# Attention and feed-forward block on one core: turning the row maxima on VectorE, splitting q and k on GpSimd, and products that nobody reads

## The reference

```
h = layernorm(x) * (1 + ca) + sa
q, k, v = h @ w_qkv.T            16 heads of width 8
a = q @ k.T / sqrt(8)            512 x 512 for each head
z = a - max(a over keys)
s = 1 + z(1 + z/2 (1 + z/3))             where z >= 0
s = 1 / (1 - z(1 - z/2 (1 - z/3)))       elsewhere (z <= 0 here)
x = x + ga * ((s / sum(s)) @ v @ w_out.T + b_out)
h = layernorm(x) * (1 + cb) + sb
x = x + gb * ffn(h)              128 -> 512 -> 512 -> 128, relu, weights +1 or -1
```

## Time and profile before

| | |
|---|---|
| median of 3 runs | 790.41 us (789.8 to 790.81) |
| the profiled execution | 786.48 us |
| its span, first to last instruction | 784.6 us |
| busy share of the span | PE 83%, PEld 31%, DVE 84%, ACT 75%, POOL 75% |
| granted TensorE clock, mean | 0.915 |

### The profile page before, as it was taken

One profiled execution on the slowest core, in us unless ns is written; L12 is line 12 of the kernel. 1 busy time (PEld: TensorE's weight loads), 2 busy tenths in 40 slices (PEclk: granted clock), 3 DMA queues, 4 the chain that ended last, 5 costly groups with the idle time before them and its releaser, 6 DMA issues.

```text
span 784.6 us, 9551 instructions
## 1 busy us (share of the span) xinstructions
PE 654.2 (83%) x2897; PEld 242.1 (31%) x2897; DVE 660.6 (84%) x806; ACT 590.3 (75%) x539; POOL 584.9 (75%) x348
## 2 busy tenths in 40 slices
PE   4377777877889998899989898899879999997877
PEld 2132222222222343223322342234322342242244
DVE  6779999798989999999989998999989999985020
ACT  2036688686897889888888889888888889899411
POOL 6227697588976999589968997789967987889310
PEclk9555669677999999999999999999999999999989
DMA  4523112410233113411331123411341120001000
GB/s 147 169 77 126 42 49 81 151 50 12 64 90 129 46 49 98 155 48 50 98 117 47 48 61 83 151 48 49 85 155 48 48 78 16 8 9 45 13 18 13
DMA packets 41110, 56.35 MB, mean 72 GB/s; under 512 B 7852, under 2 KB 24516, under 8 KB 41060
## 3 DMA queue, kind: packets, MB, share of 16 engines
q1 hardware_dynamic: 40388, 54.44, 23.2%
q10 hardware_dynamic: 672, 1.31, 0.5%
HBM read 32.06 MB, written 18.89 MB: 65 GB/s over the span
## 4 chain that ended last, share of the span: by engine, by line
PE 44%; DVE 24%; issue 15%; ACT 14%; DMA 1%; ACTq 0%; DVEq 0%; POOL 0%; POOLq 0%
DVE mx L712 12%; PE MB L417 10%; DVE cub L701 9%; PE OP L499 8%; PE SA L478 8%; PE Z L458 7%; ACT prob L552 5%; ACT sq L541 5%; PE MB L426 3%; PE SA L417 2%; PE MB L391 2%; ACT hid L582 2%; PE SA L426 1%; PE MB L394 1%; PE MB L410 1%
## 5 line engine op out<-in xcount | busy, mean ns | idle before, releaser
L844 POOL TENSOR_TENSOR cub<-cub 128x2048 f32<-128x2048 f32 x128 | 460.3, 3604 | 111.4 <-DVE cub L701 111.4
L541 ACT ACTIVATE sq<-Z,shift 128x1024 f32<-128x1024 f32 x256 | 282.9, 1117 | 110.9 <-PE Z L458 108.8
L712 DVE TENSOR_REDUCE mx<-SA 128x2 f32<-128x1024 f32 (+1 forms) x278 | 307.0, 1105 | 35.9 <-PE SA L478 34.6
L701 DVE SCALAR_TENSOR_TENSOR cub<-sq,Z 128x1024 f32<-128x1024 f32 x256 | 309.5, 1210 | 12.1 <-ACT sq L541 10.8
L552 ACT ACTIVATE prob<-cub 128x2048 f32<-128x2048 f32 x128 | 244.2, 1910 | 0.0
L478 PE MATMUL SA<-KH,QL 64*128 64x512 f32 x496 | 145.7, 523 | 62.3 <-DVE mx L712 51.4
L458 PE MATMUL Z<-QH,KH 64*128 64x512 f32 x512 | 139.8, 536 | 28.9 <-DVE cub L701 28.0
L499 PE MATMUL OP<-prob,Vq 128*16 128x512 f32 x1024 | 145.1, 641 | 1.4 <-ACT OT L590 1.4
L458 PEld LDWEIGHTS Z<-QH,KH 64*128 64x128 f32 x512 | 52.5, 199 | 222.3 <-DVE cub L701 145.7
L417 PE MATMUL MB<-hid,W 128*128 128x512 f32 x216 | 119.3, 640 | 0.0
L478 PEld LDWEIGHTS SA<-KH,QL 64*128 64x128 f32 x496 | 56.6, 200 | 162.0 <-DVE mx L712 132.1
(11 more groups left out here) (113 smaller groups left out, 396.4 us busy)
## 6 DMA issues: line engine op xcount, KB each, us to landing
parts_q<-SQ SPq DMA_DIRECT2D x32, 256.0 KB, 2.6
QL<-parts_q SPq DMA_DIRECT2D x64, 128.0 KB, 2.7
QH<-parts_q SPq DMA_DIRECT2D x64, 128.0 KB, 2.8
KH<-parts_k SPq DMA_DIRECT2D x62, 128.0 KB, 2.7
parts_k<-SK SPq DMA_DIRECT2D x28, 256.0 KB, 2.6
nd<-OT SPq DMA_DIRECT2D x128, 32.0 KB
xa<-L_attn_x SPq DMA_DIRECT2D x8, 256.0 KB, 4.2
QH<-mp SPq DMA_DIRECT2D x128, 4.0 KB
```

The costliest lines, as they stand in the source:

```text
L541: nc.scalar.activation(sq[:, h, :], Z[:, h, :], ACT.Square, bias=shift[:, 0:1]).then_inc(s_sq, 1)
L701: nc.vector.scalar_tensor_tensor(cub[:, m % RING, h, :], sq[:, h, :], CUB_ADD, Z[:, h, :], ALU.add, ALU.mult).then_inc(s_cv, 1)
L712: nc.vector.tensor_reduce(to, unit_bank(m, u)[:, heads[0]:heads[-1] + 1, :], AX_X, ALU.max)\
L844: nc.gpsimd.tensor_tensor(ff, ff, ff, ALU.mult).then_inc(s_fp, 1)
```

## The change

- **Maxima.** PE's transposing product and `alone` are gone. In steps 1, 5, 9 and 13 DVE makes the coarse and the fine part from `mx` in SBUF into a new tensor `ms` ([128 x 16] each; the first behind the first cubic, the second behind the first reduction) and turns them over with its own transpose of 32 x 32 blocks behind the second cubic ([128 x 32] into `mp`). SP writes the rows with eight DMAs of 2 KB, each of 16 runs of 128 bytes, in place of four of 4 KB.
- **q and k.** From batch 1 on ACT copies q (and k) whole into the second slot of `SQ` (`SK`), and POOL makes both parts from it in steps 1 and 2: a multiply-add copy and a subtraction, [128 x 512] each. k's product moves from place "d" to place "c" of step 1, and POOL's copy of v for the third quad from step 1 to 3.
- **Normalising on POOL.** Mean times root is made first and its sign turned (two [128 x 4] operations more), and the [128 x 128] operations become multiply, then add.
- **Last batch.** x1, y, h2T, l0 and l1_0 of `MISC[7]` and the second roots (`rs2`) move up by up to one step; in the tail l1_1 is spread over steps 0 and 1 and l1_2 goes to step 4.
- **Products that nobody reads** (`fill`): up to two a step of [128 x 128] by [128 x 512], into `MB`, in steps 10 to 15 ahead of batch 0, in 13 steps of batch 0 and 10 of batch 1. v of batch 0 moves from step 13 to 2.

```
+MISC[FIRST] = [("hT", 1, [(0, "c", 4)]), ("q", 1, [(0, "d", 4)]), ("k", 1, [(1, "d", 4)]), ("v", 1, [(2, "c", 4)])]
+FILL = {(FIRST, n): ("v", 1) for n in range(10, H)}
+FILL |= {(0, n): ("k", 2) for n in range(2, 13)} | {(0, n): ("v", 2) for n in (14, 15)}
+FILL |= {(1, n): ("k", 3) for n in range(2, 8)} | {(1, n): ("x1", 1) for n in range(9, 13)}
-    ("x1", -1, [(8, "c", 4)]),
-    ("y", -2, [(9, "c", 1), (9, "d", 1), (10, "c", 1), (10, "d", 1)]),
-    ("h2T", -1, [(11, "d", 4)]),
+    ("x1", -1, [(8, "a", 4)]),
+    ("y", -2, [(9, "a", 1), (9, "c", 1), (9, "d", 1), (10, "a", 1)]),
+    ("h2T", -1, [(10, "d", 4)]),
-AT[B - 1] = MAIN_AT | {"w2g": 4, "mv2": 9, "rs2": 10, "x1n": 10}
+AT[B - 1] = MAIN_AT | {"w2g": 4, "st2": 8, "mv2": 8, "rs2": 9, "x1n": 9}
...
+            def fill():
+                if (b, n) in FILL:
+                    name, count = FILL[b, n]
+                    pe.wait_ge(s_taken[name], count)
+                    pe.wait_ge(s_wts, 1)
+                    nc.tensor.matmul(MB[:, :], ident[:, :], W1[:, n % KC, :], start=True, stop=True)
...
             m = s + AHEAD
             scores(s + 1, 0)
-            if alone(m):
-                logits(m, 0, (1,))
             misc("a")
-            logits(m, 1, (0, 1))
+            logits(m, 1)
             with_v(s)
             scores(s + 1, 1)
             misc("c")
-            maxima_across(m)
-            logits(m + 1, 0, (0,) if alone(m + 1) else (0, 1))
+            fill()
+            logits(m + 1, 0)
             misc("d")
+            fill()
...
+            def of_maxima(m, stage):
+                raw = mx[:, i, :].rearrange("p (e c) -> p e c", e=2)
+                if stage == 0:
+                    nc.vector.tensor_scalar(ms[:, i, :, 0, :], raw, -1.0, None, ALU.mult).then_inc(s_mh, 1)
+                elif stage == 1:
+                    nc.vector.scalar_tensor_tensor(ms[:, i, :, 1, :], raw, -1.0, ms[:, i, :, 0, :].bitcast(F32),
+                                                   ALU.mult, ALU.subtract).then_inc(s_ml, 1)
+                else:
+                    nc.vector.transpose(mp[:, i, :], ms[:, i].rearrange("p e a c -> p (e a c)").bitcast(F32))\
+                        .then_inc(s_mp, 1)
...
+                nc.gpsimd.tensor_tensor(nm[:, :], mv[:, :, 0], rs[:, :], ALU.mult).then_inc(s_nm, 1)
+                nc.gpsimd.tensor_scalar(nm[:, :], nm[:, :], -1.0, 0.0, ALU.mult, ALU.add).then_inc(s_nm, 1)
-                    last = nc.gpsimd.tensor_scalar(dst[:, t, :], src[:, t, :], mv[:, t, 0:1], rs[:, t:t + 1],
-                                                   ALU.subtract, ALU.mult)
+                    last = nc.gpsimd.tensor_scalar(dst[:, t, :], src[:, t, :], rs[:, t:t + 1], nm[:, t:t + 1],
+                                                   ALU.mult, ALU.add)
+            def parts_of(beta, name):
+                pool.wait_ge(s_taken[name], beta + 1)
+                nc.gpsimd.tensor_scalar(src[:, 0, :], src[:, 1, :].bitcast(F32), 1.0, 0.0, ALU.mult, ALU.add)\
+                    .then_inc(s_hi, 1)
+                nc.gpsimd.tensor_tensor(src[:, 1, :], src[:, 1, :].bitcast(F32), src[:, 0, :].bitcast(F32), ALU.subtract)\
+                    .then_inc(s_lo, 1)
...
-                    for a in range(PARTS):
-                        r = ROWS * e + R_MAX + a
-                        sp.dma_start(QH[r:r + 1, 2 * g:2 * g + 2, :].bitcast(F32), mp[2 * TB * e:2 * TB * (e + 1), quad % 2, a, :].bitcast(F32))\
+                    for k in range(P // 32):
+                        of = 32 * k + QUAD * TB * e
+                        sp.dma_start(rows_g[r:r + PARTS, :, :, k, :].bitcast(F32), mp[of:of + QUAD * TB, quad % 2, :])\
                             .then_inc(s_mrow[g], 16)
```

More of the change, by code:

```diff
@@ L55 @@
 LOADS = 4
+M_DMAS = 8
 FIRST = -1
@@ L74 @@
 ]
-MISC = {b: MAIN for b in range(FIRST, B - 1)}
+MISC = {b: MAIN for b in range(B - 1)}
+MISC[FIRST] = [("hT", 1, [(0, "c", 4)]), ("q", 1, [(0, "d", 4)]), ("k", 1, [(1, "d", 4)]), ("v", 1, [(2, "c", 4)])]
 MISC[B - 1] = [
@@ L465, in logits @@
                 beta, g, r, qt = logits_at(m, u)
[L466 to L476, removed]
-                    rows = slice(ROWS * e, ROWS * (e + 1))
[L478 to L484, removed]
+                if m == 0 and u == 0:
+                    pe.wait_ge(s_gate, 1)
+                if m % QUAD == 0 and u == 0:
+                    pe.wait_ge(s_qk[g], (beta + 1) * LOADS * 16)
+                need(pe, s_mx, unit_before(m, u))
+                for e in range(2):
+                    rows = slice(ROWS * e, ROWS * (e + 1))
+                    mm = nc.tensor.matmul(unit_bank(m, u)[:, e, :], QL[rows, 2 * g + r, qt * P:(qt + 1) * P],
+                                          KH[rows, 2 * g + r, :], start=True, stop=True)
+                mm.then_inc(s_a, 1)
             def with_v(s):
@@ L567, in take @@
                             need(act, s_parts[name], beta * 4 * 16)
-                            nc.scalar.activation(dst[:, 0, :], bank, ACT.Copy, scale=SCALE if name == "q" else 1.0)\
-                                .then_inc(s_hi, 1)
+                            scale = SCALE if name == "q" else 1.0
+                            if beta == 0:
+                                nc.scalar.activation(dst[:, 0, :], bank, ACT.Copy, scale=scale).then_inc(s_hi, 1)
+                            else:
+                                nc.scalar.activation(dst[:, 1, :].bitcast(F32), bank, ACT.Copy, scale=scale)\
+                                    .then_inc(s_taken[name], 1)
                         elif name == "v":
@@ L702, in cubic, with maxima @@
                                                    ALU.add, ALU.mult).then_inc(s_cv, 1)
-            def maxima(m, u, heads):
+            def maxima(m, u):
                 if not 0 <= m < GROUPS:
@@ L790, in dve_step @@
             cubic(s, 0)
-            take_maxima(m)
-            if alone(m):
-                maxima(m, 0, (0,))
-                maxima(m, 0, (1,))
-            else:
-                maxima(m, 0, (0, 1))
+            of_maxima(m, 0)
+            maxima(m, 0)
+            of_maxima(m, 1)
             split(b, n)
@@ L800, in dve_step @@
             cubic(s, 1)
-            maxima(m, 1, (0, 1))
+            of_maxima(m, 2)
+            maxima(m, 1)
             take(b, n, "a")
@@ L865, in pool_step @@
                 nc.gpsimd.tensor_scalar(x1k[:, :, :], x1[:, :, :], 1.0, 0.0, ALU.mult, ALU.add).then_inc(s_x1k, 1)
-            if n in (1, 5):
-                v_in(b, 2 if n == 1 else 3)
+            if n in (1, 2) and 0 <= b < B:
+                parts_of(b + 1, "qk"[n - 1])
+            if n in (3, 5):
+                v_in(b, 2 if n == 3 else 3)
             if n in (14, 15):
```

67 lines of the change are left out of this document (38 added, 29 removed), and 10 rows, old and new, of tables (MAIN, MISC).

## The result

The change makes the kernel slower: 825.76 us median (823.22 to 827.72, 4 runs) against 790.11 us for the kernel before on the same chip (786.38 to 790.81, 4 runs), a ratio of 1.046 with a 95% interval of 1.041 to 1.050. The forecast was 777.0 us, range 745 to 806, so both its sign and its range are wrong. The traced execution has a span of 825.9 us against 784.6, 41.3 us more.

The account below looks back on a forecast made before the run. DVE's list was taken to hold the 8.8 us a batch beyond PE's sixteen 4.80 us steps. Terms of -6.0 - 4.4 - 1.2 + 0.2 - 3 + 1 = -13.4 us took the median 790.4 to 777.0 us, range 745 to 806.

Parts of the forecast that it names:

- turning the maxima, no port wait: Steps 1, 5, 9 and 13: short DVE operations replace the old turning, gaining 1.0 us a quad, 4.0 a batch.
- q and k split by POOL: Batches 0 to 6: DVE loses two operations and the waits before them, gaining 2.0 us a batch.
- port wait of both parts: Steps 1, 5, 9 and 13: DVE's SBUF operation waits for POOL's instruction, costing 4.0 us a batch, bounds 0 and 5.4.
- gather: Step 6: eight SP issues make the gather late and ACT waits, costing 0.8 us a batch, bounds 0 and 3.
- the sign that the profile would show: DVE's first part in steps 1, 5, 9 and 13 would last 1 to 2.5 us and end with POOL's instruction.
- the fine part at no wait: DVE's subtraction of two SBUF tensors, beside POOL's squares, was charged no port wait in the sum.
- the first rival: Steps 9 and 13: DVE also waits at its second part, 2.4 us each, 4.8 a batch, 806 us; chance 0.27.
- The coarse part's wait: DVE's first part waits for POOL 1.3 us in steps 1, 5 and 13 and 0.1 us in step 9.
- The rival for it: Slow issues of short runs make ACT wait over 3 us for the gather: +2.2 a batch, 792 us; chance 0.08.
- Normalising: POOL's eight operations go from 0.80 to about 0.3 us, off the path; at 0.80, 1.2 us a batch more.
- Unread products: Filled PE places raise the clock: batch 1 -4.4 us, batch 0 -1.2 together with other terms, ahead of it +1.
- The last batch: Three quads with the port wait, the gather's cost and a shorter x1n on POOL: +0.2 us together.

Follow-up runs that it names:

- twelfth: The sixth's kernel with q and k split by ACT and VectorE as before and POOL's copy of v back in step 1: 762.6 us, ratio 0.966.
- sixth: The changed kernel with both parts of the maxima by negating reductions and SP's gathers issued ahead of the rows of maxima: 743.13 us, ratio 0.941.
- third: The changed kernel with SP's four gathers issued ahead of the eight rows of maxima: 798.6 us, ratio 1.012.
- first experiment: The changed kernel with both the coarse and the fine part of the maxima made by negating reductions: 763.99 us, ratio 0.969.
- eighth: The kernel before with one unread [128 x 16] subtraction of two SBUF inputs added on DVE per quad: 826.51 us, ratio 1.048.
- second: The changed kernel with only the coarse part by a negating reduction, the fine part staying a two-tensor subtraction: 799.64 us, ratio 1.012.
- eleventh: The changed kernel with only the fine part by a negating reduction, the coarse part staying a one-input scalar operation: 814.49 us, ratio 1.030.
- tenth: The sixth's kernel with the normalising by subtract and multiply as before, without the small operations for the negated mean: 737.96 us, ratio 0.936.
- ninth: The sixth's kernel without the products that nobody reads: 749.34 us, ratio 0.949.
- fifth: The changed kernel with the maxima turned as before, by TensorE and by VectorE out of the matmul bank: 781.19 us, ratio 0.992.
- fourth: The kernel before with one unread [128 x 16] SBUF-to-SBUF tensor_scalar added on DVE per quad: 823.66 us, ratio 1.042.

## Why the prediction was wrong

Its terms for a batch at full clock, beside what the pairs of kernels above measured (means of batches 2 to 6):

| term | predicted | measured | from |
|---|---|---|---|
| turning the maxima, no port wait | -4.0 | -3.7 | twelfth 82.0 against before 85.7 |
| q and k split by POOL | -2.0 | -2.6 | sixth 79.4 against twelfth 82.0 |
| port wait of both parts | +4.0 | +8.0 | third 87.4 against sixth 79.4 |
| gather | +0.8 | +3.7 | after 91.1 against third 87.4 |
| sum | -1.2 | +5.4 | after 91.1 against before 85.7 |

The split of the last two costs depends on the order in which they are taken away: the other way round the port waits are +9.0 (after 91.1 against first 82.1) and the gather +2.7 (first 82.1 against sixth 79.4). The row of the maxima also holds what the twelfth's other differences from the kernel before do. The two gains were sized well, and the mechanism of the port wait was right, down to the sign that the profile would show (a short operation that ends with POOL's). The costs were too small, and that made a forecast of faster out of a change that is slower.

- **The step that failed: the fine part at no wait.** The sum charged the wait to the coarse part alone and left the fine part to the first rival, at 0.27, because no row showed a DVE operation with two SBUF inputs beside a square. The eighth experiment shows 1.50 us for one, the second 0.89 on the mean and 3.40 in step 9, against 0.18 as a reduction. Made quick by itself, it takes 3.5 us off a batch (after 91.1, eleventh 87.6). The Trainium skill, page "SBUF — State Buffer", section "Who interferes with whom", gives this case a sentence of its own beside the first: a DVE instruction with two SBUF inputs contends with a GpSimd instruction that reads SBUF. The trace agrees in both cases, with ends 0.03 to 0.04 us after POOL's. The rival named steps 9 and 13 and 2.4 us each; it is step 9 alone, with 3.35 in batches 3 and 4 and 0.96 to 2.11 in 2, 5 and 6, and step 13 has its wait in the coarse part.
- **The coarse part's wait was nearly right.** I had 1.3, 1.3, 0.1 and 1.3 us in steps 1, 5, 9 and 13; in batch 3 the operation took 1.25, 1.99, 0.22 and 1.53, of which 0.16 each is its own work. The row was the right one to reason from. Yet the waits' lengths are not what they cost. In the third experiment's batch 3 both parts take 7.4 us in the steps where they wait, 0.8 of it their own work, and the pair of kernels gives 8.0. Step by step (batch 5) the 1.25 us of step 1 cost 0.4, while steps 10 and 11, where no short operation stands, take 1.8 more, at the lower clock. The sum had no term for what a wait of DVE does to TensorE's clock in a batch that had run at 1.00. So it is partly luck that the waits' total lies near the cost.
- **The gather was mis-sized.** "About 6 us late" was close: from step 5's first cubic to the end of the last gather's issue are 13.8 us (341.17 to 355.01), before 7.4 (333.7, five steps behind the batch's start at 306.2, to 341.13). What failed is "idle of ACT can hide most of it": the 3.45 us of idle that it makes lie ahead of the root and the squares in ACT's list, and DVE stands 2.20 of them. Idle elsewhere in the batch doesn't hide a wait at the head of a list. The rival for it (+2.2 a batch, 0.08) had the size nearly right, and its ground was another one: transfers of 16 short runs cost 0.67 us an issue, no more than the 0.70 of the long ones. It is the number of issues and their place ahead of the gather.
- **Two rivals at once.** They were priced one at a time, and both came. The time that the first gives (806) and the gather's 15 us on top are 821 us; 825.8 were measured. That nearness is partly luck too, for the forecast was also 13.6 us off in the last batch, which neither rival has.
- **Normalising** went to 0.45 us, between the 0.3 and 0.8 of the text, and is hidden in full: at 0.80 it adds nothing in the sixth kernel (tenth), where I had 1.2 us a batch.
- **Unread products.** -4.4 for batch 1 became +1.8, since the waits lie there too; without them it is 78.7 us, 10.1 below, of which 6.3 are the products' (ninth). -1.2 for batch 0 became -0.1, and in the sixth the batch is 78.3. The fill lifted the clock (0.66 to 0.90, 0.79 to 0.92); it is worth 6.3 us in batch 1 and between nothing and some 2 us in batch 0, where DVE is busy nearly throughout.
- **The last batch: +0.2 predicted, +13.8 measured** (to the end of the last cubic). Part of it is the waits; but 5.3 stay in the sixth and 5.7 in the fifth, which has the old maxima. So they belong to what all three share, the moves of x1, y and their like by a step, or POOL's order. The traces show where: step 8 takes 8.2 us in both, before 4.8, and step 10 takes 7.0 and 6.7, before 3.5, while step 9 gives 1.3 to 1.6 back. In the sixth's step 8 DVE waits 1.48 us for the unit that PE now makes behind x1's product, and then takes x1 and makes the statistics, which lay in the next step before; PE stands 2.94 us behind that, its clock falls to the lower level for 3.4 us from 652.0, and step 10 follows. No run moved these products back alone: which of the moves costs it stays open. The tail gave 2.7 of the 3 us forecast.

## What to carry to other kernels

Before an operation on VectorE is moved from PSUM to SBUF, look at what GpSimd runs beside it and at the form of the operation: in this kernel a tensor_scalar or a two-input operation of 16 elements stood for the rest of a 3.6 us product, and a reduction of the same bytes didn't. Such a wait is busy time of one instruction, so it is found by comparing its duration with its size, not in the idle column. Look too at what TensorE's clock does behind it: here the clock fell in every steady batch that had such a wait. And when transfers are added to a hand-ordered queue, ask of each one behind them what its reader has queued after it: moving the gather in front cost nothing and gave 21 to 27 us.

## What the runs showed that I hadn't expected

- A VectorE reduction with its source in SBUF takes 0.16 us (one input) or 0.18 us (two interleaved slots by one access pattern) beside a running GpSimd product of 3.6 us; the 32 x 32 block transpose of [128 x 32] takes 0.20 to 0.22. None of the three waits: in the first experiment at least 22 of the 32 of each reduction and 10 of the 32 transposes lie wholly inside a running product of GpSimd, and the longest of each takes 0.18, 0.19 and 0.22 us.
- One added [128 x 16] operation a quad is dear: 32 x (1.49 - 0.16) = 42 us more of busy time on DVE became some 35 us of the kernel's time, though DVE was busy only 84% of the span. It isn't that each wait falls whole on the path. In batch 5 of the fourth experiment the 1.36 us of step 1 cost nothing beside the kernel before and the 1.53 of step 5 cost 0.6; but the 2.52 of step 13 cost 1.5, and step 14 behind it 1.0 more, with the clock at the lower level for 3.4 us from 574.9.
- TensorE's granted clock, 1.00 through nearly all of batches 2 to 6 before, fell to half in each of them with the waits (371.5 to 381.7 us in batch 3), each time behind idle stretches of TensorE, and didn't fall there in the first and sixth experiments. The fifth shows its price alone: with the same instructions before it, step 2 takes 6.3 us behind a fall and 4.8 without one. A small wait of TensorE can thus cost more than its length.
- GpSimd's tensor_scalar on [128 x 128] with two per-row operands takes 0.80 us as subtract and multiply and 0.45 as multiply and add.
- SyncE needs 0.65 to 0.67 us for each issue of a small SBUF to SBUF transfer of 2 KB in 16 runs, and 0.67 to 0.70 for one of 4 KB in one row.
